# Holding back the weighted sums of a quarter's last three key tiles until they can go in one run

## What is computed

```python
q = (query @ Wq.T).reshape(B, L, H, D) * scale
k = (key @ Wk.T).reshape(B, -1, H, D)
v = (value @ Wv.T).reshape(B, -1, H, D)
scores = sigmoid(einsum('blhd,bshd->bhls', q, k))
o = einsum('bhls,bshd->blhd', scores, v).reshape(B, L, E)
x = x + o @ Wo.T
# then: layer norm, top-64 tokens of each expert, gelu(g) * u, down, scatter-add, and a shared expert
```

## Time and profile before

| | before |
|---|---|
| median of three runs | 1366.16 us |
| the profiled execution | 1361.12 us, of which the span from first to last instruction 1359.3 |
| TensorE busy | 1320.3 us (97%) |
| ScalarE busy | 981.3 us (72%) |
| VectorE busy | 631.8 us (46%) |
| GpSimd busy | 283.5 us (21%) |
| sigmoids (L735) | 832, mean 1041 ns |
| score matmuls (L1396) | 1664, mean 448 ns |
| weighted-sum matmuls (L1420) | 3328 records, mean 600 ns |

### The profile page before, as it was taken

The page is one execution under the profiler, slowest core; times in us unless marked ns, Lnnn a source line. Parts: engine busy times, 40 slices in busy tenths (PEclk is TensorE's granted clock), DMA queues, the critical chain, the costliest instruction groups (busy, mean ns, idle before and its releaser), DMA issues.

```text
span 1359.3 us, 22554 instructions
## 1 busy us (share of the span) xinstructions
PE 1320.3 (97%) x8834; PEld 755.1 (56%) x8834; DVE 631.8 (46%) x1249; ACT 981.3 (72%) x1137; POOL 283.5 (21%) x286
## 2 busy tenths in 40 slices
PE   4899999999999999999999999999999999999997
PEld 3444344444444444444444443324888888888886
DVE  4353254235226335423522531211658777777762
ACT  3568988888888888888888889997232445555553
POOL 1000020002002002000200200220000466777645
PEclk9999999999999999999999999999999999999999
DMA  6466784587388478458738836833433567877754
GB/s 162 137 142 154 126 161 138 114 143 192 104 138 181 143 116 171 138 115 143 190 104 140 184 105 92 144 126 109 156 124 124 186 191 177 200 191 190 185 109 47
DMA packets 119433, 196.85 MB, mean 145 GB/s; under 512 B 22752, under 2 KB 71904, under 8 KB 119328
## 3 DMA queue, kind: packets, MB, share of 16 engines
q1 hardware_dynamic: 99456, 161.44, 50.0%
q0 software_dynamic: 19584, 33.59, 12.7%
q10 hardware_dynamic: 288, 0.39, 0.2%
HBM read 118.99 MB, written 61.83 MB: 133 GB/s over the span
## 4 chain that ended last, share of the span: by engine, by line
PE 89%; ACT 5%; DVE 2%; issue 1%; SPq 1%; DMA 1%; POOL 0%; POOLq 0%; DVEq 0%; ACTq 0%
PE acc L1420 25%; PE score L1458 19%; PE score L1396 18%; PE score L1476 9%; PE misc L1304 6%; PE misc L1317 6%; ACT probs L735 5%; PE misc L1340 2%; PE misc L1325 2%; SPq L471 1%; PE misc L1332 1%; DMA keys<-key_parts 0%; PE misc L1355 0%; DMA xn<-x 0%; DVE key_parts L851 0%
## 5 line engine op out<-in xcount | busy, mean ns | idle before, releaser
L735 ACT ACTIVATE probs<-score 128x1024 f32<-128x1024 f32 (+1 forms) x832 | 788.6, 1041 | 131.3 <-PE score L1396 125.1
L1420 PE MATMUL acc<-probs,values 128*32 128x512 f32 (+1 forms) x3328 | 412.4, 600 | 1.4 <-ACT probs L735 0.4
L1396 PE MATMUL score<-queries,keys 48*128 48x512 f32 (+1 forms) x1664 | 311.6, 448 | 4.1 <-DMA keys<-key_parts 2.9
L1396 PEld LDWEIGHTS score<-queries,keys 48*128 48x128 f32 (+1 forms) x1664 | 126.7, 180 | 261.1 <-ACT probs L735 200.4
L1420 PEld LDWEIGHTS acc<-probs,values 128*32 128x32 f32 (+1 forms) x3328 | 81.0, 108 | 181.6 <-issue 135.4
L618 POOL DMA_DIRECT2D ctx_raw<-ctx_t x32 | 23.4, 732 | 684.0 <-DVE ctx_lo L840 683.2
L744 ACT ACTIVATE gelu<-score 128x512 f32<-128x512 f32 x96 | 56.6, 599 | 96.5 <-PE score L1458 95.0
L678 POOL DMA_INDIRECT gathered<-norm_scr,gather_row x64 | 80.8, 1262 | 204.5 <-DVE gather_row L1116 189.3
L1458 PE MATMUL score<-tok_hi,gu_hi 128*128 128x512 f32 x384 | 119.2, 391 | 0.0
L1458 PE MATMUL score<-tok_lo,gu_hi 128*128 128x512 f32 x384 | 118.5, 390 | 0.0
L1458 PE MATMUL score<-tok_hi,gu_lo 128*128 128x512 f32 x384 | 118.3, 389 | 0.0
(11 more groups left out here) (185 smaller groups left out, 1430.3 us busy)
## 6 DMA issues: line engine op xcount, KB each, us to landing
keys<-key_scr SPq DMA_DIRECT2D x180, 200.2 KB, 9.2
key_scr<-key_parts SPq DMA_DIRECT2D x45, 512.0 KB, 5.0
gu_raw<-w_gu SPq DMA_DIRECT2D x17, 1024.0 KB
ctx_raw<-ctx_t POOLq DMA_DIRECT2D x24, 512.0 KB, 4.2
queries<-query_scr SPq DMA_DIRECT2D x180, 64.0 KB, 2.8
d_raw<-w_d SPq DMA_DIRECT2D x17, 512.0 KB
query_scr<-query_parts SPq DMA_DIRECT2D x15, 512.0 KB, 4.8
norm<-xn SPq DMA_DIRECT2D x224, 32.0 KB
```

The costliest lines, as they stand in the source:

```text
L735: act.activation(probs[0:rows, n % RING, 2 * pair:2 * pair + 2, :], score[k % 3][0:rows, :, :], ACT.Sigmoid, scale=SCALE).then_inc(probs_d ...
L1396: mm = pe.matmul(score[k % 3][0:rows, g, :], keys[quarter % KEY_RING][of, pair, P * st:P * st + rows], queries[half][of, e, pair, :], star ...
L1420: mm = pe.matmul(acc[32 * c:32 * (c + 1), :], values[b % 2][0:rows, st, half, c, :], probs[0:rows, n % RING, c, :], start=(st == 0), stop= ...
```

## The change

`sums_after` gets one more condition. When exactly three tiles of a quarter are still to be summed (`done % NST == NST - 3`) and fewer than three are due, none goes at this quad. So tiles 10, 11 and 12 of such a quarter go together once all three are due. Quarters where the plan's pairs end elsewhere (11 tiles done, or 12) are as before.

```diff
     for n in range(QUADS):
         upto = n - LAG + 1
         if n % QPB in BESIDE[n // QPB] and upto - done < 2:
             upto = done
+        if done % NST == NST - 3 and upto - done < 3:
+            upto = done
         upto = max(done, min(upto, NST * (done // NST + 1)))
         plan.append(range(done, upto))
         done = upto
```

## The result

The changed kernel took 1387.62 us in the median (1379.78 to 1390.25), the kernel before beside it 1366.66 (1365.29 to 1367.49): ratio 1.0149, 95% interval 1.0123 to 1.0175. That is 21.0 us slower. Forecast were +12.3 us and 1378.4, with a range up to 1383. The direction was right and the price of the blocks too, as will be seen. Most of the missing 8.7 us came from something that the prediction had put aside with 2%, the lower clock of TensorE in batch 7; a smaller part from batch 0.

What follows compares the result with a forecast made beforehand. Bound: TensorE while projections are mixed in, ScalarE's sigmoid in batch 7. Sum: 3.6 + 5.1 + 1.5 + 2.6 + 0.9 - 1.5 + 0.1 = +12.3 us, so 1378.4 us in the median; range 1373.5 to 1383.

Steps and rivals of the forecast that it cites:

- batch 0: Quads 13 to 17: second K no longer waits for the copy of `misc`, -1.5 us; quads 26 and 27, +0.1.
- (a): Quads 12 to 14 of batches 1 to 6: a score block waits for its bank; +0.60 us each, +3.6.
- (b): Last quad of batches 0 to 5 and next two: removed run wholly replaced by waiting; +0.85 us each, +5.1.
- (c): End of batch 6, where batch 7 begins with no projection: third score block waits for its bank; +1.5 us.
- (d): Batch 7, quads 12 to 14 and 38 to 40: ScalarE stands still for 1.0 us; +1.3 each, +2.6.
- (e): Quads 25 to 27 of batch 7, with the short gate product between: ScalarE rests longer; +0.9 us.
- Rivals 1 and 2: Rival 1: banks free in time, only removed runs count, -2.9 us, 3%. Rival 2: waits in (a), (b) hidden, +1.9, 4%.
- Rival 3: Smaller throughout: run of three at its lower bound, waits in (d) made up; +6 to +7 us, 7%.
- rival 4: Larger: shifted key transfers or the `probs` ring cost 1 us more at each of 12 places; 1390 us, 3%.
- rival 5: TensorE's clock falls for the run after each rest at 20 places: 20 x 2.6 us more, about 1430; 2%.

Runs made afterwards that it cites:

- the last profile: Whole change plus idle matmuls in batch 0's waits and batch 7's six gaps: 1376.24 us, 13.4 above the kernel before with its waits filled.
- a single empty gap: Kernel before, with the last two tiles held instead of three, at three places only (end of batch 6, two in batch 7): 1367.36 against 1364.98 us.

## Why the prediction was right and wrong

**The price of the blocks: right.** A run of three takes 2.71 to 2.72 us; it was taken as 2.72. The release of a bank (end of the sigmoid's record plus 0.05) gave +0.60 and +0.85 for (a) and (b); measured were 0.60 to 0.64 and 0.84 to 0.86 in the changed kernel's profile and, over all twelve places, 8.7 to 9.0 for the predicted 8.7. (c), (d) and (e) without a fall: 1.55 to 1.58, 1.35 to 1.39 and 0.74 to 0.81, for 1.5, 1.3 and 0.9. Batch 0: -1.6 for -1.5, in the profile. With the waits filled on both sides the whole change measured +13.4 for +12.3. The signs named in the prediction came too: batches 1 to 5 each longer by 1.43 to 1.49 us in the changed kernel's profile, for 1.45, and in the last profile ScalarE rests 1.00 to 1.02 us at the four places of batch 7, for about 1. One did not: batch 0 is not shorter in the changed kernel's profile.

**Rivals 1 and 2 fall** with that: the banks don't come free in time, and a run's 0.14 us is lost several times over in each place of (a) to (e). The Trainium skill, "TensorEngine Tiling (Array Packing)", Key Properties, says that changing the tiling mode drains TensorE. The rows agree that a run has a price of its own, 0.14. That fewer changes are then better is the prediction's own step, and it doesn't hold here: what lay between two score blocks was also the time in which ScalarE emptied a bank.

Rival 3 falls with the run of three at 2.71, rival 4 with the twelve places at 8.7 to 9.0.

**The clock: the step that failed.** The sum priced every block at full clock and gave the lower clock nothing. That was rival 5, at 2%, put aside with the sentence that in batch 7 S waits for its bank in nearly every quad, and the clock stays up. The rows were right, the transfer wasn't. Before, TensorE was busy for 96.98 of 98 us there. An S that waited took 911.54 - 910.70 = 0.84 in place of 0.65, so 0.2 us a quad, with a sum behind each:

```profile
910.70 0.91 PE L1396 MATMUL score<-queries,keys 48*128 48x512 f32 x4
```

The changed order has four rests in a row with score blocks alone between them: 0.47, 0.30, 0.41 and 0.41 at (c), 1.59 of the 4.20 us from 853.60 to 857.80, and the like at (d), of 0.21 to 0.57. That is another pattern, of which no row told. The price of one fall was right in size, 2.6 for 5.28 - 2.71 = 2.57 at (d), though over the five falls it ran from 1.4 to 4.1. But the rival was counted at every one of 20 places (about 1430) or not at all, where some places in some executions is what came; and by the plan the runs of three are 18, not 20, and at the twelve of (a) and (b) the clock never fell. In the changed kernel's profile the falls of batch 7 cost 3.24 - 1.58, 5.44 - 1.37 and 2.91 - 1.39, together 7.3 us.

The Trainium skill, "TensorE: Matmul & The Clock Gate", A second HAM failure mode: psum-queue depth-cycling, says that short idle times between groups of matmuls, while PSUM buffers cycle, can make the clock swing between its two levels. The runs agree, with rests of 0.21 to 0.57 us at the places that fell.

**The second term: batch 0.** The sum took 1.5 us off for it. In the five profiles with the rule there and nothing filled there the gain is 0.0 to 0.1 us, with half clock at that place in each. With 7.3 for the clock in batch 7, 12.3 for the blocks and these 1.5 put back it is 21.1, for 21.0 measured. That it comes out so closely is luck, since the places are one execution's and the 21.0 is a difference of medians.

**The sum was made against an execution that was lucky.** The profiled one took 1361.12, 5.0 us under the median; it had no half clock in the first 95 us, which the prediction didn't note (it said that the two stand 5 apart, and left it there). That didn't spoil the forecast, since the median was shifted with it. But of the ten profiles with nothing filled in batch 0, all but this one have a stretch of half clock in the first 95 us. So this execution's rows could not show how easily the clock falls, and the clock in every slice was no typical one.

**What stays open.** Why the whole change fell at three places in one execution and at one in another: these experiments don't show what decides it. It is open too whether falls come more rarely with the rule in batch 7 alone (+6.0 us, its places 5.1) than with the whole change (+19.8 and +21.0, its places 12.3), or only seemed to on that chip. The last comparison, +13.4, stands 1.1 over the sum, of which the two profiles show nothing in the attention (12.24). And how often a single empty gap brings the clock down: the one profile of it shows no fall, and its +2.4 us for 1.7 of places leaves little room for many.

## What to carry to other kernels

An operation between two producers of the same ring of buffers is not only work: it is the time in which the consumer empties a buffer. Before joining two short runs into one longer, work out what stands in the gap that is left, by the release of the buffer three steps back; here a run saved 0.14 us, and an emptied gap cost 0.5 to 0.9 net. And where an order adds rests to TensorE, price the lower clock in some of the executions, place by place; two idle matmuls in the rest are a cheap test of it, and were here the remedy for part of the loss.

## What the runs showed of the hardware

Filling TensorE's waits in the first 80 us with matmuls that compute nothing made the kernel before 4.4 us faster (1362.85 against 1367.23). With the rule in batch 0 it was 4.2 (1361.01 against 1365.20, on another chip): the ratio is 0.9967 in both, so no order between these two is shown. The spread, 10.9 and 6.5 us for the unfilled kernel of these two sets, shrank to 2.6 and 1.7. The half clock at 60 to 100 us, which eight of the ten unfilled profiles have, is in none of the three kernels so filled; here the one with the rule in batch 0 (a stretch at about 31 us stayed in the two others):

```profile
60.00:100.00 40.00, 39.76 (x266) 20.52 (x266) 20.32 (x49) 27.16 (x30) 2.16 (x3) 1.00 0.67 147
```

A second thing went with it: where nothing was filled, seven of ten profiles had the keys of quad 13 land some 2.2 us late (6.0 to 6.4 us from the scores of quad 12 to those of 13, in place of 3.85; a wait of 3.76 us in the changed kernel in place of the 1.57 before). All seven have half clock at 60 to 100 us, of the three others one. In the three filled ones the keys were never late. Whether that comes with the fillings or by chance was not tried, so what part of the 4.4 us is the clock's and what part the keys' is open.
